# A sparsemax attention stage: order of the queues around the threshold rounds, and the threshold's rounds by rows

## The reference

```python
def sparsemax(x):
    x = x - jnp.max(x, axis=-1, keepdims=True)
    zs = -jnp.sort(-x, axis=-1)
    rho = jnp.arange(1, L + 1, dtype=x.dtype)
    cssv = jnp.cumsum(zs, axis=-1) - 1.0
    support = zs > cssv / rho
    k = jnp.maximum(jnp.sum(support, axis=-1, keepdims=True), 1)
    tau = jnp.take_along_axis(cssv, k - 1, axis=-1) / k.astype(x.dtype)
    return jnp.clip(x - tau, 0.0)
...
scores = jnp.einsum('bhqd,bhkd->bhqk', qh, kh) * scale     # 2 x 16 heads, 512 queries, 1024 keys
attn = sparsemax(scores)
out = jnp.einsum('bhqk,bhkd->bhqd', attn, vh)
```

## Time and profile before

| | us |
|---|---|
| median of 3 runs (lowest to highest) | 3412.17 (3408.17 to 3413.89) |
| the profiled execution, its own time | 3412.49 |
| its span, first to last instruction | 3410.7 |
| TensorE, weight loads, VectorE, ScalarE, GpSimd busy | 2470.1, 1570.8, 2040.2, 1425.7, 423.8 |
| first candidates to last output copy of the sparsemax stage | 779.3 to 1544.1 |

### The profile page before, as it was taken

The page is one execution under the profiler, slowest core; times in us unless marked ns, Lnnn a source line. Parts: engine busy times, 40 slices in busy tenths (PEclk is TensorE's granted clock), DMA queues, the critical chain, the costliest instruction groups (busy, mean ns, idle before and its releaser), DMA issues. The chain is left out here.

```text
span 3410.7 us, 37710 instructions
## 1 busy us (share of the span) xinstructions
PE 2470.1 (72%) x12065; PEld 1570.8 (46%) x12066; DVE 2040.2 (60%) x4897; ACT 1425.7 (42%) x2245; POOL 423.8 (12%) x228
## 2 busy tenths in 40 slices
PE   2999995363666666654799277877884996899598
PEld 1444443241333333323799145545433884454387
DVE  4666662857777777733465345565654556675377
ACT  1555551113888777861344122122351222266121
POOL 0000000011000000001675120211100111200021
PEclk8999998675777777766899689988886997799799
DMA  1001102043011111001564200000521111531010
GB/s 59 21 24 25 26 17 78 17 131 96 1 26 26 26 26 26 7 1 47 181 202 145 80 0 0 0 0 11 149 51 34 45 31 64 156 86 32 30 42 31
DMA packets 87781, 174.61 MB, mean 51 GB/s; under 512 B 23560, under 2 KB 52240, under 8 KB 84176
## 3 DMA queue, kind: packets, MB, share of 16 engines
q1 hardware_dynamic: 86096, 168.64, 16.9%
q0 software_dynamic: 1536, 4.20, 0.4%
HBM read 133.41 MB, written 38.99 MB: 51 GB/s over the span
## 5 line engine op out<-in xcount | busy, mean ns | idle before, releaser
L1497 ACT ACTIVATE l1a_over_s<-l1a_sc_s,l1a_minus_step_s 128x1024 bf16<-128x1024 f32 x256 | 290.0, 1140 | 3.0 <-DVE l1a_minus_step_s L1371 1.7
L1311 DVE MAX8 l1a_cand_s<-ps 128x8 f32<-128x128 f32 x1024 | 213.2, 282 | 69.0 <-PE ps L1206 65.1
L1239 PE MATMUL ps<-l1a_probs_s,l1h_v_s 128*32 128x256 f32 x1024 | 123.3, 570 | 159.8 <-ACT l1a_probs_s L1505 158.5
L1483 ACT ACTIVATE l1a_sc_s<-ps,l1a_minus_tau_s 128x1024 f32<-128x1024 f32 x128 | 142.0, 1112 | 140.3 <-DVE l1a_minus_tau_s L1340 53.1
L1024 DVE TENSOR_REDUCE l3a_shift_s<-ps 128x1 f32<-128x1024 f32 x128 | 150.1, 1219 | 51.1 <-PE ps L941 51.1
L1206 PE MATMUL ps<-l1h_ka_s,l1h_qa_s 128*128 128x512 f32 x256 | 132.2, 559 | 56.1 <-DVE l1a_cand_s L1311 45.5
L1085 ACT ACTIVATE l3a_probs_s<-ps 128x512 f32<-128x512 f32 x256 | 132.7, 603 | 88.9 <-PE ps L957 88.7
L1962 PE MATMUL ps<-m1e_x_part_s,m1e_up_part_s 128*128 128x256 f32 x1152 | 151.7, 289 | 13.6 <-POOL m1e_up_part_s L2142 12.0
L1962 PEld LDWEIGHTS ps<-m1e_x_part_s,m1e_up_part_s 128*128 128x128 f32 x1152 | 144.4, 196 | 17.0 <-POOL m1e_up_part_s L2142 15.0
L1505 ACT ACTIVATE l1a_probs_s<-ps 128x1024 f32<-128x1024 f32 x128 | 125.7, 1016 | 62.7 <-PE ps L1227 62.7
L646 ACT ACTIVATE l0a_probs_s<-ps 128x1024 f32<-128x1024 f32 x128 | 124.1, 1021 | 53.6 <-PE ps L482 52.0
(11 more groups left out here) (575 smaller groups left out, 5509.8 us busy)
## 6 DMA issues: line engine op xcount, KB each, us to landing
m1e_up_s<-m_up SPq DMA_DIRECT2D x32, 768.0 KB, 4.4
m1e_down_s<-m_down SPq DMA_DIRECT2D x16, 768.0 KB, 4.6
l1h_ka_s<-l_k_parts SPq DMA_DIRECT2D x16, 512.0 KB, 8.0
l3h_ka_s<-l_k_parts SPq DMA_DIRECT2D x16, 512.0 KB, 8.0
l0a_w_s<-l_w SPq DMA_DIRECT2D x16, 384.0 KB, 3.1
m3ew_up_s<-m_up SPq DMA_DIRECT2D x6, 768.0 KB, 4.3
l0a_rden_s<-l0a_rden_rows SPq DMA_DIRECT2D x32, 128.0 KB, 2.9
m_sorted<-ones SPq DMA_DIRECT2D x1, 4096.0 KB, 16.5
```

The lines of the kernel that those rows point to most:

```text
L1239: ins = nc.tensor.matmul(ps[32 * h:32 * h + 32, VALUES, 0:HALF], v[:, n % 2, t, h, :], probs[:, t % 4, h * HALF:(h + 1) * HALF], start=(t ...
L1311: ins = nc.vector.max(cand[:, r, 8 * (c + j * 4):8 * (c + j * 4) + 8], ps[:, A0 + f % 2, c * P:(c + 1) * P])
L1483: nc.scalar.activation(sc[:, r, :], ps[:, PAIR + 2 * (place % 2):PAIR + 2 * (place % 2) + 2, :].rearrange("p a n -> p (a n)"), ACT.Relu, b ...
L1497: nc.scalar.activation(over[:, done % 2, :], sc[:, r, :], ACT.Relu, bias=minus_step[:, r:r + 1], accum_out=total[:, i, r:r + 1]).then_inc( ...
```

## The change

- TensorE: `first_banks` makes the next unit's scores bank by bank instead of row by row. Pairs 0 and 1 of the next unit and the first two banks of the one after it move ahead of the end of a unit; one bank stands between pairs; banks 10 and 11 beside tiles 0 and 1, banks 12 to 15 behind the products of tile 2. `turn` becomes `turn_worst`, behind tile 7, and `turn_shift`, at the end.
- VectorE: `first_threshold` becomes `begin_threshold`, `better_threshold` (one round) and `end_threshold`. Running sums by doubling in three steps; each round by eight row instructions that count and eight that sum, all with accumulators, the unused output in bf16. Two rows of the next unit's candidates go ahead of `cut`; the begin and the first round of the next unit go ahead of `third_threshold`, the other two behind it.
- ScalarE: rounds 1 and 2 in halves (`SUMS`): rows 0 to 3 ahead of tiles 2 and 5, rows 4 to 7 ahead of tiles 3 and 6.

```diff
+    SUMS = {2: (1, 0, 4), 3: (1, 4, 8), 5: (2, 0, 4), 6: (2, 4, 8)}
+    BESIDE_AGAIN = ((3, 4), (4, 5), (5, 6), (6, 7), (7, 8), (8, 10))
...
-        cand, above = s.sb("cand", [P, ROWS, CAND]), s.sb("above", [P, ROWS, CAND])
-        best, ranks = s.sb("best", [P, ROWS, 8]), s.sb("ranks", [P, 8])
+        cand, above = s.sb("cand", [P, ROWS, CAND]), s.sb("above", [P, 2, ROWS, CAND], BF16)
+        best, ranks = s.sb("best", [P, 2, ROWS, 12]), s.sb("ranks", [P, 8])
...
-            def first_row(u, r):
+            def first_banks(u, begin, end):
+                if u >= UNITS:
+                    return
                 n = u // 2
...
+                for r, j in [divmod(f, NH) for f in range(begin, end)]:
+                    buf, h, at = where(u, r)
+                    if u % 2 == 0 and r == 0 and j == 0:
...
-            def turn(u):
+            def turn_worst(u):
                 pe.wait_ge(worst_ready, u + 1)
                 if u > 0:
                     pe.wait_ge(lo_ready, u)
                 nc.tensor.transpose(ps[0:1, TURN, 0:P], worst[:, :], ident[:, :]).then_inc(worst_turned, 1)
+
+            def turn_shift(u):
                 pe.wait_ge(settled, u + 1)
                 nc.tensor.transpose(ps[0:ROWS, TURN, 0:P], shift[:, u % 2, :], ident[:, :]).then_inc(shift_turned, 1)
 
...
-            for r in range(ROWS):
-                first_row(0, r)
+            first_banks(0, 0, FIRST)
+            again(0, 0)
+            first_banks(1, 0, 2)
+            again(0, 1)
             for u in range(UNITS + 1):
-                for r in range(ROWS):
-                    if u < UNITS:
+                if u < UNITS:
+                    first_banks(u + 1, 2, 3)
+                    for r in range(2, ROWS):
                         again(u, r)
-                    if r == 1 and u > 0:
-                        turn(u - 1)
-                    if u + 1 < UNITS and 2 <= r < 6:
-                        first_row(u + 1, r - 2)
+                        first_banks(u + 1, *BESIDE_AGAIN[r - 2])
                 if u == UNITS - 1:
                     denominators(0)
                 for t in range(NC_):
                     if u > 0:
                         second(u - 1, t)
-                    if u + 1 < UNITS and t < 4:
-                        first_row(u + 1, 4 + t)
+                    if t < 2:
+                        first_banks(u + 1, FIRST - 6 + t, FIRST - 5 + t)
                     if u == UNITS and t < PARTS[0][1]:
                         spread_bank(t)
+                    if t == NC_ - 1 and u < UNITS:
+                        turn_worst(u)
                     if u > 0 and t > 0:
                         value_products(u - 1, t - 1)
+                    if t == 3:
+                        first_banks(u + 1, FIRST - 4, FIRST)
+                if u + 1 < UNITS:
+                    again(u + 1, 0)
+                    first_banks(u + 2, 0, 2)
                 if u > 0:
                     value_products(u - 1, NC_ - 1)
+                if u + 1 < UNITS:
+                    again(u + 1, 1)
+                if u < UNITS:
+                    turn_shift(u)
...
-            def first_threshold(u):
+            def begin_threshold(u):
 
                 k = u % 2
                 dve.wait_ge(rows_used, FIRST * (u + 1))
                 nc.vector.sem_inc(seen, 1)
                 for r in range(ROWS):
-                    own.done(nc.vector.max(best[:, r, :], cand[:, r, :]))
+                    own.done(nc.vector.max(best[:, 0, r, 4:12], cand[:, r, :]))
                 own.done(nc.vector.reduce_max(last[:, :], cand[:, :, :].rearrange("p r (c e) -> p r c e", e=8)[:, :, :, 7],
                                               AX.X))
                 own.wait()
-                for j in range(1, 8):
-                    own.link(nc.vector.tensor_tensor(best[:, :, j], best[:, :, j], best[:, :, j - 1], ALU.add))
-                own.link(nc.vector.scalar_tensor_tensor(best[:, :, :], best[:, :, :], -1.0,
+                for i, by in enumerate((1, 2, 4)):
+                    a = best[:, i % 2, :, :]
+                    own.link(nc.vector.tensor_tensor(best[:, 1 - i % 2, :, 4:12], a[:, :, 4:12], a[:, :, 4 - by:12 - by],
+                                                     ALU.add))
+                sums_of = best[:, 1, :, 4:12]
+                own.link(nc.vector.scalar_tensor_tensor(sums_of, sums_of, -1.0,
                                                         ranks[:, :].unsqueeze(1).to_broadcast([P, ROWS, 8]),
                                                         ALU.add, ALU.mult))
-                own.link(nc.vector.reduce_max(tau[:, k, :], best[:, :, :], AX.X))
-                for i in range(MICHELOT + 1):
-                    own.link(nc.vector.tensor_tensor(above[:, :, :], cand[:, :, :], wide(tau[:, k, :], CAND), ALU.is_gt))
-                    own.link(nc.vector.reduce_sum(number[:, k, :], above[:, :, :], AX.X))
-                    if i < MICHELOT:
-                        own.done(nc.vector.tensor_tensor(above[:, :, :], above[:, :, :], cand[:, :, :], ALU.mult))
-                        own.link(nc.vector.reciprocal(rcount[:, :], number[:, k, :]))
-                        own.link(nc.vector.reduce_sum(slope[:, :], above[:, :, :], AX.X))
-                        own.link(nc.vector.scalar_tensor_tensor(tau[:, k, :], slope[:, :], -1.0, rcount[:, :],
-                                                                ALU.add, ALU.mult))
+                own.link(nc.vector.reduce_max(tau[:, k, :], sums_of, AX.X))
+
+            def count_above(u):
+                k = u % 2
+                for r in range(ROWS):
+                    own.done(nc.vector.tensor_scalar(above[:, 0, r, :], cand[:, r, :], tau[:, k, r:r + 1], 0.0,
+                                                     ALU.is_gt, ALU.add, accum_out=number[:, k, r:r + 1]))
+
+            def better_threshold(u):
+                k = u % 2
+                count_above(u)
+                for r in range(ROWS):
+                    own.done(nc.vector.scalar_tensor_tensor(above[:, 1, r, :], cand[:, r, :], tau[:, k, r:r + 1],
+                                                            cand[:, r, :], ALU.is_gt, ALU.mult,
+                                                            accum_out=slope[:, r:r + 1]))
+                own.wait()
+                own.link(nc.vector.reciprocal(rcount[:, :], number[:, k, :]))
+                own.link(nc.vector.scalar_tensor_tensor(tau[:, k, :], slope[:, :], -1.0, rcount[:, :],
+                                                        ALU.add, ALU.mult))
+
+            def end_threshold(u):
+                k = u % 2
                 nc.vector.tensor_scalar(minus_tau[:, k, :], tau[:, k, :], -1.0, None, ALU.mult).then_inc(tau_set, 1)
+                count_above(u)
                 own.link(nc.vector.tensor_tensor(last[:, :], last[:, :], tau[:, k, :], ALU.subtract))
                 own.link(nc.vector.tensor_scalar(last[:, :], last[:, :], 0.5, 5e-7, ALU.mult, ALU.max))
                 own.link(nc.vector.reciprocal(rgap[:, k, :], last[:, :]))
...
+                more = u + 1 < UNITS
+                if more:
+                    candidates(u + 1, 0)
+                    candidates(u + 1, 1)
                 if u > 0:
                     cut(u - 1)
-                if u + 1 < UNITS:
-                    for r in range(ROWS // 2):
+                if more:
+                    for r in range(2, 5):
                         candidates(u + 1, r)
                 second_threshold(u)
-                if u + 1 < UNITS:
-                    for r in range(ROWS // 2, ROWS):
+                if more:
+                    for r in range(5, ROWS):
                         candidates(u + 1, r)
+                    begin_threshold(u + 1)
+                    better_threshold(u + 1)
                 third_threshold(u)
-                if u + 1 < UNITS:
-                    first_threshold(u + 1)
+                if more:
+                    for i in range(1, MICHELOT):
+                        better_threshold(u + 1)
+                    end_threshold(u + 1)
                 else:
...
-            def sums(u, i):
+            def sums(u, i, begin, end):
                 act.wait_ge(step_set, 2 * u + i)
                 if i == 1:
                     act.wait_ge(pair_used, again_place(u, ROWS - 1) + 1)
-                for r in range(ROWS):
+                for r in range(begin, end):
...
-                    if u < UNITS and t == 2:
-                        sums(u, 1)
-                    if u < UNITS and t == 4:
-                        sums(u, 2)
+                    if u < UNITS and t in SUMS:
+                        sums(u, *SUMS[t])
```

More of the change, by code:

```diff
@@ L1192, in _ @@
         def _(pe):
[L1193 removed]
+            def first_banks(u, begin, end):
+                if u >= UNITS:
+                    return
                 n = u // 2
[L1195 to L1202 removed]
+                for r, j in [divmod(f, NH) for f in range(begin, end)]:
```

(7 more changed lines are left out.)

16 lines of the change are left out of this document (6 added, 10 removed).

## The result

The changed kernel takes 3420.61 us (median of 8 runs, 3419.80 to 3422.61) against 3412.02 (8 runs, 3408.17 to 3414.46) for the one before: ratio 1.0028, 95% interval 1.0017 to 1.0039. It is slower, by 8.6 us. The prediction said slower by 64. The profiled execution took 3420.37, with a span of 3418.5 and a mean clock of 0.831.

A forecast was written before the change was run, and what follows sets the result against it. Two queues taking turns bound the kernel: ScalarE in the rounds, VectorE with TensorE's order at the hand-over. Fourteen units +65, start +2.7, unit 0 -0.2, unit 15 -4.5: total +63, 3412.5 to 3476 us, range 3400 to 3505.

The forecast's parts named there:

- The round by rows: VectorE's threshold rounds as 16 row instructions at p = 0.27 us: a round 4.8 against 3.2 us, a loss.
- P: Period of a steady unit, from first sums to the next first sums: 48.9 us, 4.7 above 44.25.
- both bounds: P is the larger of 41.9 + 16p (ScalarE ends last) and 33.9 + 56p (VectorE does), crossing at p = 0.20.
- the first rival: No separate accumulator write-out on VectorE: p = 0.197, P = 45.05, time 3414 us; chance 0.14.
- The read: On VectorE, an accumulator's write-out as its own instruction behind each row instruction, taken as 0.075 us.
- The head: First sums on ScalarE: one bank between TensorE's pairs, first pair made early; eight sums 9.1 us, a gain.
- The gap: Banks 12 to 15 wait behind tile 2's products; VectorE idles from 12.6 to 18.2 us, a loss.
- The order on VectorE: begin_threshold and one round of the next unit ahead of third_threshold: ScalarE idle some 8 us ahead of round 2, a loss.
- The rounds: Round 2's sums with tile 5 take 9.97 us; VectorE ends last, settling starts 2.7 us after the last sum.
- the sign of a p too large: VectorE finishing the threshold before ScalarE's last sum would show p below 0.2 and the forecast wrong.
- Hand-over: From the settling's start s to the next first sum: 5.1 us, TensorE's queue taking the place of the flag's wait.
- Edges: Outside the steady units: ahead of unit 0 +2.7 us, unit 0 -0.2, unit 15 -4.5.

The follow-up runs named there:

- e4: Changed kernel with groups of eight row instructions ahead of the stage, with and without accumulator, threshold from memory or constant: SCALAR_TENSOR_TENSOR 0.207 against 0.197 us.
- e2: Changed kernel with banks 12 to 15 ahead of tile 2's products in TensorE's queue: 3347.18 us, 0.9796 of the kernel before.
- e1: Changed kernel with third_threshold directly behind the candidates, begin_threshold and all three rounds of the next unit behind it: 3420.45 us, 1.0024 of the kernel before.
- e7: Changed kernel with ScalarE's rounds 1 and 2 whole ahead of tiles 2 and 4, not in halves: 3517.62 us, 1.0307 of the kernel before.
- e8: Changed kernel with banks 12 to 15 ahead of tile 2's products and ScalarE's rounds whole: 3375.82 us, 0.9892 of the kernel before.
- e10: Kernel before with only TensorE's order at a unit's end changed, first two pairs made ahead of turn_shift: 3400.78 us, ratio 0.9959.
- e12: Kernel before with only ScalarE's tiles spread among the sums, each round in two halves: 3405.68 us, ratio 0.9977.
- e3: Changed kernel with the threshold's rounds over 128x512 as before, instead of row instructions: 3410.54 us, 0.9991 of the kernel before.
- e5: Changed kernel with banks 12 to 15 ahead of tile 2's products and the old threshold rounds over 128x512: 3336.16 us, 0.9776 of the kernel before.
- e11: Kernel before with only the threshold's rounds changed to row instructions with accumulators: 3429.50 us, ratio 1.0052.
- e9: Kernel before with rounds by rows, but the new tau step left out of all rounds but the last, so the fallback ran every unit: 10553.16 us.

## Why the prediction was right in sign and wrong in size

The step that failed is "The round by rows": "I take 0.197 + 0.075 = 0.27". Measured, p, the time from the start of one row instruction to the next, is 0.200 for TENSOR_SCALAR and 0.207 for SCALAR_TENSOR_TENSOR, and the accumulator's share of it, taken as 0.075, is 0.01 in the second (e4). Put into the prediction's own formulas, p = 0.20 gives P = 45.1 (both bounds meet there) and the time of the first rival, 3414 to 3415; measured are 45.14 and 3420.6. The 3.8 us between P = 48.9 and 45.1 all come from this one term, since p is multiplied by 56 instructions a unit. That rival denied a separate read; the record shows one. Its time is right and its reason is not: the read is there and lies over its neighbour. The right sign is in part luck: at p = 0.20 the formulas give 2 to 3 us more than before, which no measurement here would tell from nothing. The measured 8.6 is 4.6 inside the stage, with two misses at its edges that nearly cancel (below), and the rest outside it.

- *The read.* It is a recorded instruction of 82 ns, as predicted from ScalarE's pairs and from MATCH_VALUE_LOAD. But the next row instruction starts with it, and e4 prices it at 0.01. I took a record's duration for its cost. The Trainium skill (VectorE: DVE Perf Modes, section "Two Vector instructions with no wait between them") says that such an instruction is two, the main one and an accumulator read; the trace agrees (a read of 82 ns behind each).
- *The head.* Predicted 9.1 for the eight first sums, measured 8.72.
- *The gap.* Predicted 5.6 us of idle time ahead of bank 12, measured 5.45; end of the candidates at 21.9 predicted, 1098.13 - 1076.15 = 21.98 measured. e2 shows what it is worth.
- *The order on VectorE.* `begin_threshold` predicted 2.64, measured 1100.74 - 1098.13 = 2.61; from the third threshold to ScalarE 1.68 and 1106.20 - 1104.55 = 1.65. ScalarE's wait was foreseen with 8 us, measured 7.35. e1 shows that this wait is no loss of its own, so "loses" was wrong for this step in the kernel as measured.
- *The rounds.* Settling was to start 2.7 us after the last sum. It starts 0.21 after it (1116.38): the two queues end together, as the formulas have it for p = 0.20. The prediction had named an end of the threshold ahead of the last sum as the sign of a p too large. Its sentence that the tiles spread among the sums don't shorten the unit does not hold either: taking the spread back costs 97 us in the changed kernel (e7) and 29 with the gap closed (e8).
- *Hand-over.* s + 5.1 predicted, 1121.68 - 1116.38 = 5.3 measured, with TensorE's queue in the flag's place.
- *Edges.* Unit 15 was to gain 4.5 and gained 6.3: its tile 0 starts 2.9 us sooner after the first sum than before, which was not counted, and the rest gives 1.2 less than forecast. Ahead of unit 0 the sum at p = 0.20 has -0.7, measured -0.3. Unit 0 gained 1.3, where the formula at p = 0.20 has 4.6. Most of the rest is a wait that I had not seen: bank 2 of unit 1 stands in TensorE's queue ahead of unit 0's third pair and needs VectorE, which is still in `end_threshold`:

```profile
814.31 1.11 ACT L1528 ACTIVATE l1a_sc_s<-ps,l1a_minus_tau_s 128x1024 f32<-128x1024 f32 x1 [2.58 <-PE ps L1220]
```

- *A reading.* The prediction says that ScalarE is idle ahead of tile 6 alone in the kernel before; it is idle 1.14 us ahead of tile 7 as well (the row under e7). No term of the sum uses it.

So the mechanism was right in the main, and the number failed by one duration. The gap is a loss of 5.3 us a unit (e2). The new hand-over with the pairs made ahead is a small gain (e10, P 0.9 shorter), the moved tiles another (e12, P 0.6 shorter), and the rounds by rows are a small loss (e3, e5, e11). These gains do not add up to the whole: with the gap closed and the old rounds (e5) P is 44.25 - 39.24 = 5.0 shorter than before, of which e10 and e12 by themselves show 1.5. The rest is left to the order on VectorE, the single bank between pairs, the shorter running sums (2.61 instead of 3.30) and what these do together; no run takes them apart.

## What to carry to other kernels

Price an instruction of a stream by the time from its start to the next one's start, not by the records that appear beside it: a recorded helper can lie wholly over its neighbour. Where one term is repeated tens of times a period, the forecast should be stated as a function of it, with the point at which the bounding queue changes, and the value taken should lean on the nearest start-to-start distances (here 0.197). And in an in-order queue, ask of every instruction whose result is not needed soon (here the products of tile 2) what stands behind it: moving four banks past it was worth eight times the whole effect of this change.

## What the runs showed of the hardware

In e4 a VectorE row of 64 elements with accumulator and a scalar from memory starts 0.20 us after the one before, with a constant 0.14; the accumulator adds 0.01 to a SCALAR_TENSOR_TENSOR. TENSOR_SCALAR of 128 elements with accumulator took 0.267 against 0.197 without, and e9's fallback loop has 1279 ns for 1024 elements with it, where the earlier trace rows has 753 ns without. The Trainium skill (VectorE: DVE Perf Modes, section "What auto-detection actually checks") lets an instruction with a single source and its destination in SBUF take two elements at a time; the trace agrees for TENSOR_SCALAR without accumulator, and shows that with one the gain is gone.

In these runs a MEMSET on GpSimd holds some VectorE instructions until it ends, and others not. In e4 eight rows with accumulator ran at their 0.20 while one was under way, and the eight without, which began 0.2 us ahead of its end and of three further MEMSETs, took 6.22 us instead of the 1.39 of the second time, ending (792.70) with the last of the three (792.64):

```profile
783.19 3.51 POOL L707 MEMSET l1h_ka_s<- 64x4096 f32 x1
...
784.96 0.28 DVE L1487 TENSOR_SCALAR_CACHE_REDUCE l1a_above_s<-l1a_cand_s,l1a_tau_s 128x64 bf16<-128x64 f32 x1
...
786.48 6.22 DVE L1490 TENSOR_SCALAR l1a_above_s<-l1a_cand_s,l1a_tau_s 128x64 bf16<-128x64 f32 x8
786.65 1.85 POOL L706 MEMSET l1h_qa_s<- 64x2048 f32 x1
...
788.44 3.62 POOL L707 MEMSET l1h_ka_s<- 64x4096 f32 x1
792.01 0.63 POOL L1188 MEMSET l1a_rden_parts_s<- 64x512 f32 x1
```

In e11 all five MEMSETs of the steady units held a TENSOR_SCALAR without accumulator, and with four of them the subtraction right behind it. Ahead of the last one, five rows with accumulator went by at their 0.20 while the MEMSET was already under way (1306.44 to 1307.44). The Trainium skill (GPSIMD Engine Reference, section "Specifications") says that GpSimd's interfaces to SBUF are shared with VectorE and names instructions in a two-port mode and those with two SBUF inputs; the trace agrees with it for TENSOR_SCALAR without accumulator (6.22 us) and, for the subtraction on `last`, does not tell a hold of its own from standing behind the other. In the changed kernel the same MEMSETs met MAX8 instructions that read from PSUM, and cost nothing that is seen.
